# Three instructions of ScalarE's attention stage put in another place of its queue

## The chip, the cores and the metric

One core of a Trainium2 chip runs the whole program. The metric is device time in microseconds (us), median of the runs. Five engines work beside each other, each through its own list of instructions in order: PE (matmuls and transposes, with PEld for its weight loads), DVE, ACT (ScalarE), POOL and SP. They wait for one another by counting semaphores.

## The reference

The input is x, 2048 tokens of 128 features. Two layers are computed, and the change is in the second:

```
xn = layernorm(x)
x  = x + attention(xn) + ffn(xn)                    # layer 1
  attention: q, k with a rotary half; s = q k^T, causal mask; p = softmax(s); o = p v; o wo
  ffn: h = silu(xn w1^T s1) * (xn w2^T s2)          # the gate, 512 wide
       h = gelu(h h1^T sh1); h = gelu(h h2^T sh2); h w3^T s3
```

Layer 0 (a recurrent memory, and one expert) comes first and is not touched.

## The kernel before

The second layer has two stages. The attention stage runs from about 93 to 193 us of the trace, the two 512 x 512 layers and the last one after it. The attention stage is one loop over t = 0 to 16 on every engine (NT = 16). Row t is a block of 128 queries. Its scores go in groups of four key blocks (up to 512 columns, `groups_of`), so rows 8 to 11 have three groups and rows 12 to 15 four; the last one can be shorter (row 8: 512, 512, 128; row 9: 512, 512, 256). In step t the engines do this, in this order:

- PE: the scores of row t (L906), then for row t - 1 the transposes of its first two groups ("turn round", L919), then the matmuls of this step's early gates (L879, L880), then for each group of row t - 1 the product with the values ("weighted", L929), with the turn round of the third group after the first weighted group and of the fourth after the second, then a late gate's matmuls.
- DVE: the maxima of row t's groups (L2022), the negative maximum as bias (L2029), the early gates (L2007, L2008, and from the ninth step on a cast L2014 of its own), then row t - 1: sum, reciprocal, and x += o (L2051), then a late gate, then a check of weights (L2060).
- ACT: the copies of row t - 1's turned groups out of PSUM ("turned copy", L1369), the tanh of the early gates (L1342), the exponentials of row t (L1385, each with a read of its accumulator), casts of early gates (L1397, only for steps before 8), the tanh of a late gate, and pieces of weight conversion (L1357, L1362, L1363).
- POOL: the low half of each gate (L1497, L1498), and weights.

A gate u is one of 32 pieces of 128 x 256. Steps 2 to 11 have two early gates each, steps 6 to 9 one late gate each. So gates 0 and 1 are step 2, gates 17, 18 and late 19 are step 9, gates 22 and 23 are step 11. Gates before 24 take turns in PSUM banks 3 and 6, and PE waits before a gate for the last gate in its bank (`hA_ready`, which L2008 counts up): gate 19 waits for gate 17. From row 12 (`FULL`) on bank 3 belongs to the scores, and PE's scores of row 12 wait for all 24 gates:

```
if t == FULL:

    pe.wait_ge(hA_ready, GATES_AT[FULL])
```

An exponential waits for its bias, and overwrites nothing that PE still needs; scores wait for the exponential that last read their bank. A weighted group waits for its turned copy. DVE's gate waits for its tanh. POOL's part of a gate waits for its cast.

Of the kernel before, what the change touches and what calls it, by code (L numbers as in the profile page):

```python
# [7 lines left out]
ACT = mybir.ActivationFunctionType  # L8
# [25 lines left out]
HT4 = HID // P  # L34
ROT = 64
ZC = 256
# [52 lines left out]
def program(nc, a, out):  # L89
    with ExitStack() as ctx:  # L90
# [3 lines left out]
        def sem(name):  # L94
            return ctx.enter_context(nc.semaphore(name))
# [126 lines left out]
        def second(n):  # L222
            b_at[0] += n
            return arena[:, b_at[0] - n:b_at[0]]
# [12 lines left out]
        hAH, hAL, hBH, hBL = (h[:, i * HT4 * T // 2:(i + 1) * HT4 * T // 2].bitcast(F16).rearrange("p (m t) -> p m t", m=HT4)  # L237
                              for h in (hAf, hBf) for i in range(2))
# [10 lines left out]
        TH, ZA, ZG, zd = gate_[0:3], gate_[3:6] + [second(ZC) for _ in range(3)], gate_[6], gate_[7]  # L249
        NZ = len(ZA)  # L250
# [10 lines left out]
        def weights_with(t):  # L261

            return [i for i in range(NWT) if WT_TILE[i] == t]
# [54 lines left out]
        z_done, tanh_ready, hA_ready = sem("z_done"), sem("tanh_ready"), sem("hA_ready")  # L318
# [3 lines left out]
        w16_ready, xh_act, xl_ready, gate_high, gate_low, wsq_act, wc_ready, tern_ready, rest_ready, low_ready = (  # L322
            sem(n) for n in ("w16_ready", "xh_act", "xl_ready", "gate_high", "gate_low", "wsq_act", "wc_ready", "tern_ready", "rest_ready", "low_ready"))
# [10 lines left out]
        def groups_of(t):  # L334
            before = sum((u + 4) // 4 for u in range(t))
            return [(before + k, c, min(4, t + 1 - c)) for k, c in enumerate(range(0, t + 1, 4))]


        FULL = 3 * NT // 4
        SCORE_BANK = [gi % (3 if t < FULL else 4) for t in range(NT) for gi, _, _ in groups_of(t)]  # L340
        SCORE_AFTER = [max([w for w in range(gi) if SCORE_BANK[w] == SCORE_BANK[gi]], default=None) for gi in range(len(SCORE_BANK))]

# [4 lines left out]
        GATE_EARLY = [range(u, u + n) for u, n in zip(GATES_AT, EARLY_GATES)]  # L347
# [3 lines left out]
        HIGH_BY_ACT = {u for t in range(HIGH_TILES) for u in GATE_EARLY[t]}  # L351
# [77 lines left out]
        def _(sp):  # L429
# [30 lines left out]
            for k, (_, n0, cnt) in enumerate(RESULTS):  # L460
                if k == BY_ACT:
                    continue
                sp.wait_ge(out_ready, k + 1)
                sp.dma_start(out_dram[:, n0:n0 + cnt, :], fin[:, n0:n0 + cnt, :]).then_inc(out_sem, 16)
# [575 lines left out]
        def _(act):  # L1040
            f = nc.scalar.activation
# [255 lines left out]
            def high(c):  # L1297

                f(xH[:, c * BANK:(c + 1) * BANK], xT[:, c * BANK:(c + 1) * BANK], ACT.Copy).then_inc(xh_act, 1)
# [35 lines left out]
            def tanh(u):  # L1335

                act.wait_ge(z_done, u + 1)
                if u == 0:
                    act.wait_ge(scales_ready, 2)
                if u >= 3:  # L1340
                    act.wait_ge(hA_ready, u - 2)
                f(TH[u % 3], PS[:, GATE_BANK[u], 0:ZC], ACT.Tanh, scale=s1h[:, u % HT4:u % HT4 + 1]).then_inc(tanh_ready, 1)  # L1342

            def weights(i):

                if i in (3, 7):
                    act.wait_ge(h_in[(i - 3) // 4], 16)
                if i == 0:

                    act.wait_ge(turned_dve, 4)  # L1350
                    act.wait_ge(turned_pool, 4)
                    act.wait_ge(xl_ready, 4)
                if i >= NWC:

                    act.wait_ge(tern_ready, i - NWC + 1)
                w = weights_of(i)
                f(WC[i % NWC], w, ACT.Square).then_inc(wsq_act, 1)  # L1357
                if i >= 2:
                    k = (i - 3) % 4
                    wH, wL = (q.rearrange("p m e -> p (m e)") for q in (w3H, w3L)) if i == 2 else (  # L1360
                        q[:, k, :] for q in ((h1H, h1L), (h2H, h2L))[(i - 3) // 4])
                    f(wH, w, ACT.Copy).then_inc(w16_ready, 1)  # L1362
                    f(wL, w, ACT.Copy, scale=1.0 / LOW).then_inc(w16_ready, 1)  # L1363

            def turned_back(t):

                for gi, c, cnt in groups_of(t):
                    act.wait_ge(pt_done, gi + 1)
                    f(PT[t % 2][:, c * P:(c + cnt) * P], PS[:, 4 + gi % 2, 0:cnt * P], ACT.Copy).then_inc(pt_act, 1)  # L1369
                    yield  # L1370

            for t in range(NT + 1):
                copies = turned_back(t - 1) if t else iter(())
                next(copies, None)
                next(copies, None)
                for u in GATE_EARLY[t]:
                    tanh(u)
                if t < NT:
                    if t >= 2:
                        act.wait_ge(pv_done, t - 1)  # L1380
                    act.wait_ge(bias_ready, t + 1)
                    for k, (gi, c, cnt) in enumerate(groups_of(t)):
                        if k >= 1:
                            next(copies, None)
                        f(Pr[t % 2][:, c * P:(c + cnt) * P], PS[:, SCORE_BANK[gi], 0:cnt * P], ACT.Exp,  # L1385
                          scale=1.0 / D, bias=nbs[:, t:t + 1], accum_out=rsums[:, gi:gi + 1]).then_inc(p_ready, 1)
                for _ in copies:
                    pass
                if t < 2:
                    high(t + 2)  # L1390
                for u in GATE_EARLY[t]:
                    if u in HIGH_BY_ACT:

                        act.wait_ge(hA_ready, u + 1)
                        if u:
                            act.wait_ge(gate_high, u)
                        f(hAH[:, u % HT4, u // HT4 * ZC:(u // HT4 + 1) * ZC], ZA[u % NZ], ACT.Copy).then_inc(gate_high, 1)  # L1397
                for u in GATE_LATE[t]:
                    tanh(u)
                for i in weights_with(t):  # L1400
                    weights(i)
# [749 lines left out]
```

## Time and profile before

| | |
|---|---|
| median of 3 runs | 256.38 us (256.31 to 256.75) |
| profiled execution, and its span | 256.91 us, 255.1 us |
| PE busy | 245.0 us (96%), 1669 instructions |
| DVE busy | 204.5 us (80%) |
| ACT busy | 185.8 us (73%), 460 instructions |
| POOL busy | 115.0 us (45%) |
| chain that ended last | PE 63%, DVE 20%, POOL 6%, ACT 3%, issue 3%, DMA 2% |
| granted TensorE clock | 1.0 over the span |

The span is the time from the first to the last instruction of one profiled execution; 1.8 us of its own time lie around it. The chain is followed back from the last instruction through whatever released each step.

### The profile page before, as it was taken

The page shows a single profiled execution, that of the slowest core. Times are in us where ns is not written, and L with a number is a line of the kernel's source. Part 1 is how long each engine was busy: PE and PEld are TensorE (multiplying, and loading weights), DVE is VectorE, ACT ScalarE, POOL GpSimd, SP SyncE. Part 2 cuts the span into 40 slices and gives each one's busy share as a digit, 9 for nine tenths or more (in the row PEclk, how much of TensorE's full clock was granted, in tenths as well). Part 3 has the DMA queues.
Part 4 walks back from the last instruction along what each step waited for, and adds up shares of the span by engine and source line. Part 5 has one row for each costly group of instructions (what it writes and reads, how often), then busy time and mean ns, then how long its engine had stood idle before and what let it go on. Part 6 is the DMA issues. An engine that isn't in the chain of part 4 may idle for free.

```text
span 255.1 us, 5149 instructions
## 1 busy us (share of the span) xinstructions
PE 245.0 (96%) x1669; PEld 160.1 (63%) x1673; DVE 204.5 (80%) x681; ACT 185.8 (73%) x460; POOL 115.0 (45%) x150
## 2 busy tenths in 40 slices
PE   7899998999998999999999999999999999999993
PEld 2359554776764477786778767886875444444492
DVE  7888899999958998998899887787613996666674
ACT  2697789976637887887667899989814997777730
POOL 9789700000004589887755994997790000000000
PEclk9999999999999999999999999999999999999999
DMA  6620000000008403000000000000000000000004
GB/s 189 187 81 3 1 0 3 1 0 3 3 3 321 177 15 149 3 1 0 4 0 3 0 0 3 1 1 0 4 3 0 0 0 3 0 1 0 1 29 141
DMA packets 8479, 8.50 MB, mean 33 GB/s; under 512 B 1793, under 2 KB 7554, under 8 KB 7938
## 3 DMA queue, kind: packets, MB, share of 16 engines
q1 hardware_dynamic: 7074, 7.52, 8.8%
q10 hardware_dynamic: 1376, 0.62, 0.9%
q8 instruction: 15, 0.25, 0.4%
q14 instruction: 14, 0.11, 0.1%
HBM read 7.09 MB, written 1.05 MB: 32 GB/s over the span
## 4 chain that ended last, share of the span: by engine, by line
PE 63%; DVE 20%; POOL 6%; ACT 3%; issue 3%; DMA 2%; DVEq 0%; SPq 0%; POOLq 0%; ACTq 0%
PE PS L957 11%; PE PS L956 11%; PE PS L929 8%; PE PS L906 7%; PE PS L919 4%; POOL arena L1497 3%; POOL arena L1498 3%; PE PS L718 3%; DMA x<-L_attn_x 2%; PE PS L672 2%; PE PS L726 2%; DVE mxb L2022 2%; DVE arena L2008 2%; PE PS L575 2%; PE PS L570 2%
## 5 line engine op out<-in xcount | busy, mean ns | idle before, releaser
L956 PE MATMUL PS<-arena 128*128 128x512 f16 x128 | 48.5, 379 | 0.0
L957 PE MATMUL PS<-arena 128*128 128x512 f16 x128 | 48.5, 379 | 0.0
L2080 DVE TENSOR_TENSOR arena<-arena 128x512 f32<-128x512 f32 x32 | 22.2, 693 | 13.0 <-ACT arena L1416 13.0
L906 PE MATMUL PS<-arena 128*128 128x512 f32 (+3 forms) x80 | 31.9, 530 | 0.3 <-ACT arena L1385 0.3
L1415 ACT ACTIVATE arena<-PS,arena 128x512 f32<-128x512 f32 x32 | 22.9, 715 | 9.1 <-PE PS L957 9.1
L1497 POOL TENSOR_TENSOR arena<-arena 128x256 f32<-128x256 f32 x32 | 21.5, 672 | 15.7 <-DVE arena L2014 13.1
L1385 ACT ACTIVATE arena<-PS,lnt 128x512 f32<-128x512 f32 (+3 forms) x40 | 24.8, 628 | 3.2 <-DVE lnt L2029 3.2
L1498 POOL TENSOR_TENSOR arena<-arena,small 128x256 f16<-128x256 f32 (+1 forms) x36 | 23.8, 660 | 2.8
L1505 POOL CAST arena<-arena 128x512 f16<-128x512 f32 x2 | 1.3, 637 | 49.1 <-ACT x L1278 49.1
L1416 ACT ACTIVATE arena<-PS,arena 128x512 f16<-128x512 f32 x32 | 22.8, 712 | 0.0
L2022 DVE TENSOR_REDUCE mxb<-PS 128x1 f32<-128x512 f32 (+3 forms) x40 | 22.1, 601 | 0.0
L957 PEld LDWEIGHTS PS<-arena 128*128 128x128 f16 x128 | 12.5, 98 | 14.7
L956 PEld LDWEIGHTS PS<-arena 128*128 128x128 f16 x128 | 12.5, 98 | 14.6
L906 PEld LDWEIGHTS PS<-arena 128*128 128x128 f32 x80 | 14.0, 191 | 12.0 <-issue 9.8
L919 PE MATMUL PS<-con,arena 128*128 128x128 f32 x136 | 19.5, 273 | 0.0
L929 PE MATMUL PS<-arena,xn 128*128 128x128 f32 x144 | 19.3, 278 | 0.0
L929 PEld LDWEIGHTS PS<-arena,xn 128*128 128x128 f32 x144 | 17.7, 191 | 1.1 <-ACT xn L1369 0.4
L929 PE MATMUL PS<-arena 128*128 128x128 f32 x128 | 17.4, 279 | 0.6 <-ACT arena L1369 0.6
L2051 DVE SCALAR_TENSOR_TENSOR x<-PS,lnt,x 128x128 f32<-128x128 f32 x16 | 5.6, 351 | 14.1 <-PE PS L929 13.7
L919 PEld LDWEIGHTS PS<-con,arena 128*128 128x128 f32 x136 | 15.1, 141 | 2.7 <-issue 1.9
L929 PEld LDWEIGHTS PS<-arena 128*128 128x128 f32 x128 | 15.6, 191 | 1.4 <-ACT arena L1369 1.0
L2008 DVE SCALAR_TENSOR_TENSOR arena<-PS,arena 128x256 f32<-128x256 f32 x32 | 15.5, 484 | 1.1
(292 smaller groups left out, 614.5 us busy)
## 6 DMA issues: line engine op xcount, KB each, us to landing
arena<-h_T SPq DMA_DIRECT2D x2, 1024.0 KB, 5.9
arena<-cos SPq DMA_DIRECT2D x1, 1024.0 KB, 4.8
arena<-sin SPq DMA_DIRECT2D x1, 1024.0 KB, 6.8
arena<-w_T SPq DMA_DIRECT2D x3, 256.0 KB, 3.1
x<-L_attn_x SPq DMA_DIRECT2D x2, 256.0 KB, 5.5
out<-arena SPq DMA_DIRECT2D x2, 256.0 KB, 2.2
x<-L_attn_x SPq DMA_DIRECT2D x2, 128.0 KB, 2.6
x<-L_attn_x ACTq DMA_DIRECT2D x2, 128.0 KB, 3.2
```

What stands on the lines that cost most here:

```text
L906: i = mm(PS[:, k, 0:cnt * P], qT1[:, t * P:(t + 1) * P], kT1[:, c * P:(c + cnt) * P], start=True, stop=not last)
L919: i = tr(PS[:, 4 + gi % 2, (b - c) * P:(b - c + 1) * P], Pr[t % 2][:, b * P:(b + 1) * P], ident)
L929: i = mm(PS[:, 7, (t % 4) * D:(t % 4 + 1) * D], PT[t % 2][:, b * P:(b + 1) * P], V1[:, b, :], start=(b == 0), stop=(b == t))
L956: mm(bank(b), wH[:, k, m * P:(m + 1) * P], sH[:, k, cols], start=(k == 0), stop=False)
L957: i = mm(bank(b), wL[:, k, m * P:(m + 1) * P], sL[:, k, cols], start=False, stop=(k == HT4 - 1))
L1385: f(Pr[t % 2][:, c * P:(c + cnt) * P], PS[:, SCORE_BANK[gi], 0:cnt * P], ACT.Exp, scale=1.0 / D, bias=nbs[:, t:t + 1], accum_out=rsums[:, ...
L1415: f(FP[u % 4], bank(u % 8), ACT.Gelu, scale=s_[:, u % HT4:u % HT4 + 1])
L1416: f(high, bank(u % 8), ACT.Gelu, scale=s_[:, u % HT4:u % HT4 + 1]).then_inc(read, 1)
L1497: o.need(o.did(tt(rest, value, high, ALU.subtract)))
L1498: return tt(low, rest, low_scale.broadcast_to([P, cols]), ALU.mult)
L2022: i = did(v.tensor_reduce(mxb[:, gi:gi + 1], PS[:, SCORE_BANK[gi], 0:cnt * P], AX.X, ALU.max))
L2080: v.tensor_tensor(RP[m], FP[m], high, ALU.subtract).then_inc(rest_ready, 1)
```

## The change

All three edits are on ACT, and nothing is added or removed: the same 460 instructions run in another order.

1. The cast of gate 1 (`HIGH_LATER = 2`, the second early gate of step 2) stood at the end of step 2. It now stands in step 3, behind the turned copy of row 2.
2. In step 9 (`COPY_FIRST`) the third turned copy of row 8 (128 columns) stood behind the first exponential of row 9. It now stands behind the first two copies, ahead of the tanhs of gates 17 and 18 and of all three exponentials.
3. In step 11 (`TANH_LATER`) the tanh of gate 23 stood behind that of gate 22 and ahead of the exponentials. It now stands behind the third exponential of row 11.

```
+            def high_of_gate(u):
+
+                if u in HIGH_BY_ACT:
+                    act.wait_ge(hA_ready, u + 1)
+                    if u:
+                        act.wait_ge(gate_high, u)
+                    f(hAH[:, u % HT4, u // HT4 * ZC:(u // HT4 + 1) * ZC], ZA[u % NZ], ACT.Copy).then_inc(gate_high, 1)
+
+            HIGH_LATER, COPY_FIRST, TANH_LATER = 2, 9, 11
+
             for t in range(NT + 1):
                 copies = turned_back(t - 1) if t else iter(())
                 next(copies, None)
                 next(copies, None)
-                for u in GATE_EARLY[t]:
+                if t == COPY_FIRST:
+                    next(copies, None)
+                if t == HIGH_LATER + 1:
+                    high_of_gate(GATE_EARLY[HIGH_LATER][-1])
+                behind = 1 if t == TANH_LATER else len(GATE_EARLY[t])
+                for u in GATE_EARLY[t][:behind]:
                     tanh(u)
                 if t < NT:
...
                 for _ in copies:
                     pass
+                for u in GATE_EARLY[t][behind:]:
+                    tanh(u)
                 if t < 2:
                     high(t + 2)
                 for u in GATE_EARLY[t]:
-                    if u in HIGH_BY_ACT:
...
+                    if t != HIGH_LATER or u != GATE_EARLY[t][-1]:
+                        high_of_gate(u)
```

## Rows read from the trace of the kernel before

**Rows 1.** Windows: busy us of each engine in a stretch, then granted clock.
```profile
93.00:132.00 39.00, 38.67 (x276) 30.66 (x277) 35.22 (x100) 28.88 (x80) 31.66 (x43) 1.00 0.08 28
132.00:148.00 16.00, 15.33 (x104) 11.90 (x103) 13.96 (x38) 13.32 (x36) 11.49 (x15) 1.00 0.00 1
148.00:190.00 42.00, 42.00 (x281) 32.51 (x281) 29.39 (x75) 35.02 (x83) 33.91 (x38) 1.00 0.01 1
190.00:249.00 59.00, 59.00 (x356) 30.61 (x355) 41.26 (x79) 40.54 (x65) 1.24 (x1) 1.00 0.02 5
```
**Rows 2.** Chain that ended last, in order: start, us, what.
```profile
132.71 0.49 PE PS L929 x2
...
146.48 1.35 ACT arena L1385 x4
...
147.83 3.04 PE PS L906 x8
```
**Rows 3.** Timeline, step 3: start, us, engine, line, what, count, [idle before <-releaser].
```profile
100.65 0.42 ACT L1397 ACTIVATE arena<-arena 128x256 f16<-128x256 f32 x1 [0.63 <-DVE arena L2008]
100.97 0.47 ACT L1369 ACTIVATE arena<-PS 128x384 f32<-128x384 f32 x1
101.49 0.74 PEld L929 LDWEIGHTS PS<-arena 128*128 128x128 f32 x6 [0.49 <-ACT arena L1369]
101.70 0.15 DVE L2029 TENSOR_SCALAR lnt<-mxb 128x1 f32<-128x1 f32 x1
101.84 0.42 DVE L2007 SCALAR_TENSOR_TENSOR arena<-arena,PS 128x256 f32<-128x256 f32 x1
```
**Rows 4.** Timeline of ACT, step 9.
```profile
130.16 0.84 ACT L1342 ACTIVATE arena<-PS,arena 128x256 f32<-128x256 f32 x2
131.71 0.69 ACT L1385 ACTIVATE arena<-PS,lnt 128x512 f32<-128x512 f32 x1 [0.71 <-DVE lnt L2029]
...
132.39 0.27 ACT L1369 ACTIVATE arena<-PS 128x128 f32<-128x128 f32 x1
132.55 0.69 ACT L1385 ACTIVATE arena<-PS,lnt 128x512 f32<-128x512 f32 x1
```
**Rows 5.** Groups by line and form, 90 to 190 us: busy us, mean ns.
```profile
L1342 ACT ACTIVATE arena<-PS,arena 128x256 f32<-128x256 f32 x32 | 14.2, 480 | 0.1
```
**Rows 6.** Timeline of PE and its weight loads, step 9.
```profile
131.19 0.27 PE L919 MATMUL PS<-con,arena 128*128 128x128 f32 x1
...
132.71 0.30 PEld L929 LDWEIGHTS PS<-arena 128*128 128x128 f32 x2 [0.54 <-ACT arena L1369]
...
133.04 0.27 PE L879 MATMUL PS<-arena 128*128 128x256 f16 x1
```
**Rows 7.** Timeline of DVE, steps 9 and 10.
```profile
131.46 0.15 DVE L2029 TENSOR_SCALAR lnt<-lnt 128x1 f32<-128x1 f32 x1
131.58 0.42 DVE L2007 SCALAR_TENSOR_TENSOR arena<-arena,PS 128x256 f32<-128x256 f32 x1
132.04 0.48 DVE L2008 SCALAR_TENSOR_TENSOR arena<-PS,arena 128x256 f32<-128x256 f32 x1
```
**Rows 8.** Timeline of ACT and the weight loads, step 10.
```profile
138.53 0.69 ACT L1385 ACTIVATE arena<-PS,lnt 128x512 f32<-128x512 f32 x1 [0.18 <-DVE lnt L2029]
...
139.21 0.37 ACT L1369 ACTIVATE xn<-PS 128x256 f32<-128x256 f32 x1
...
138.65 1.50 PEld L929 LDWEIGHTS PS<-arena,xn 128*128 128x128 f32 x12
```
**Rows 9.** Timeline of ACT, step 11.
```profile
144.43 0.84 ACT L1342 ACTIVATE arena<-PS,arena 128x256 f32<-128x256 f32 x2
145.14 0.71 ACT L1385 ACTIVATE arena<-PS,lnt 128x512 f32<-128x512 f32 x1
...
147.70 0.64 ACT L1357 ACTIVATE arena<-arena 128x512 f32<-128x512 f32 x1
```
**Rows 10.** Timeline of DVE and the weight loads, steps 11 and 12.
```profile
144.94 0.42 DVE L2007 SCALAR_TENSOR_TENSOR arena<-arena,PS 128x256 f32<-128x256 f32 x1 [0.80 <-ACT arena L1342]
...
147.09 0.48 DVE L2008 SCALAR_TENSOR_TENSOR arena<-PS,arena 128x256 f32<-128x256 f32 x1
...
147.80 0.30 PEld L906 LDWEIGHTS PS<-arena 128*128 128x128 f32 x2 [0.48 <-issue]
```

More of the change, by code:

```diff
@@ L1391, in _ @@
                 for u in GATE_EARLY[t]:
-                    if u in HIGH_BY_ACT:
[L1394 to L1397, printed above, removed]
+                    if t != HIGH_LATER or u != GATE_EARLY[t][-1]:
+                        high_of_gate(u)
                 for u in GATE_LATE[t]:
```

## The prediction

> **What bounds the kernel now.** I read the stretches first: they say which engine has no room where the three edits stand. From 93 to 132 us DVE is busy 35.22 of 39 us and PE's rows overlap, so its 38.67 says little; from 148 us to the end of the second 512-wide layer PE is busy 42.00 of 42.00 and 59.00 of 59.00 us, without a gap [rows 1]. So whatever delays or advances PE at about 148 us moves the end by the same amount, and an edit before 132 us counts only if DVE or the hand-over to PE moves. Then I read the chain of waits in order of time. It changes from DVE to PE at 132.71 us, at the third weighted group of row 8, and at 147.83 us it enters the scores of row 12, after which it stays on PE [rows 2]. Last I read the timelines around the three places; the working below is a re-timing from them.
>
> **Edit 1, gate 1's cast behind row 2's copy: 0 to -0.1 us, I take -0.03.** Before, the cast waited 0.63 us for DVE and the copy stood behind it at 100.97 us [rows 3]. The copy's input is there at about 100.3 us, so it starts some 0.65 us earlier, the cast follows at about 100.7, where it was anyway, and the tanhs and PE's weighted group move up by some 0.4 us. PE had idled 0.49 us there [rows 3]. What takes over is DVE: gate 2 starts 0.14 us after its bias instruction at 101.70 [rows 3], and every later pair of these is 0.11 to 0.15 apart as well (0.12 in step 9 [rows 7]), so at most 0.03 us was a wait for the tanh. DVE has no other gap to give until step 6. PE is early, then waits for nothing it could not have had. The cast is no later, so nothing queued behind it (two tanhs and an exponential) is either.
>
> The chain names POOL between 97 and 114 us, which I don't follow: a gate waits for POOL's part of the gate six before it, and that was done 3 to 5 us earlier each time.
>
> **Edit 2, row 8's short copy ahead of the tanhs: +0.58 us.** What it removes: the copy at 132.39 us stood behind an exponential that waited for its bias, and PE idled 0.54 us for it, until 132.71 [rows 4, 6]. What it adds: the copy can't start before its transpose, a matmul at 131.19 of 0.27 us [rows 6], so 131.50 with the 0.04 us that such a hand-over takes. In front of that point ACT used to run both tanhs, from 130.16 on [rows 4]; they now stand in the queue behind the waiting copy, and behind them all of row 9's exponentials.
> - Copy 131.50; it holds the queue 0.16 us, as from 132.39 to 132.55 [rows 4]. The tanh of gate 17 is at 131.66 and takes 0.48 us [rows 5], to 132.13.
> - DVE's gate 17 was at 131.58, straight behind the bias [rows 7]. It now waits until 132.16: +0.58 us. It is ready 0.94 us on (0.46 to the second instruction, which takes 0.48 [rows 7]), at 133.10.
> - The second tanh is 0.36 us behind the first (0.84 less 0.48 [rows 4, 5]), and the first exponential 0.36 behind that: 132.38 in place of 131.71 [rows 4], +0.67.
> - PE gets the copy at 131.8, runs the third weighted group without its stall at 132.2, and then stands before gate 19, which waits for gate 17: 133.16 in place of 133.04 [rows 6]. The 0.54 us are gone and PE is 0.12 us later than before.
> - DVE runs the rest of step 9 and the maxima of row 10 without a gap, so the +0.58 stays: row 10's bias, and with it the exponential that waits for it at 138.53, moves to 139.11, and row 9's third copy, behind that, from 139.21 to 139.79 [rows 8].
> - PE needs that copy for the last four of twelve weight loads. They take 1.50 us where eight take 0.97 and four more 0.44: it already waited some 0.09 us for it [rows 8]. So here PE falls back the full 0.58 us.
> Bounds: +0.12 if DVE makes its delay good within row 10 (its cast of gate 18 ran 0.63 us in place of 0.29 beside POOL, which is such a place), +0.67 if the exponential's shift counts. I take 0.58, the first one that has no slack behind it.
>
> The Trainium skill, "ScalarE: Activation LUTs", Rules for kernel authors, has a budget of about 0.3 us for every ACTIVATE and 0.83 ns for an element. By it the copy would hold the queue 0.41 and the tanh 0.51 us, gate 17 would start at 132.45, and the edit would cost 0.87 us and the whole change 2.4. The trace overlaps neighbours (0.16 and 0.36 from start to start), and I stay with it.
>
> **Edit 3, gate 23's tanh behind row 11's exponentials: +1.57 us.** Before, the two tanhs ran from 144.43 and the first exponential from 145.14 [rows 9]. Without the second tanh that exponential starts 0.36 us earlier, which buys nothing: the copy behind it waits for its transpose until 145.95, so the second and third exponentials stay. The tanh goes to where the third exponential lets go of the queue, the 147.70 of the next instruction [rows 9], and ends at 148.17. DVE had gate 22 at 144.94, 0.03 us behind its tanh [rows 10]; gate 23 so starts at 148.20 and is ready at 149.14, where it was ready at 147.09 + 0.48 = 147.57 [rows 10]. The scores of row 12 wait by the code for 24 gates, this one the last; they came at 147.80, 0.23 us behind it [rows 10]. They now come at 149.37: +1.57. PE's whole queue is behind them (rows 12 to 15, then both layers), as are DVE's row 10 output and weight checks behind the gate; the weight conversions on ACT move 0.36 us and had idled 0.5 us in front of the next copy. PE is the bound from there on [rows 1], with nothing that gives time back. Bounds: the same 1.57 less the 0.23 if that was not hand-over, so +1.34, and +1.8 if the cast that follows, and runs beside POOL, holds DVE longer.
>
> **Sum.** Edit 3's path starts from PE's transposes of row 10, so edit 2's delay adds to it: -0.03 + 0.58 + 1.57 = +2.12 us. From the profiled execution's 256.91 us (span 255.1) that gives 259.0 (span 257.2). The median shown is 0.53 us below the profiled one, so I forecast 256.38 + 2.12 = 258.5 us. Its own range is 258.1 to 258.9.
>
> **The rivals.**
> - *Only edit 3 costs (18%).* DVE makes up for step 9 in steps 10 and 11 (it idles 0.80 us in step 11 [rows 10]), and PE keeps up to all of the 0.54 us it wins [rows 6], or loses 0.12. For it: the idle time is there. Against it: the hand-over in step 10 comes before that idle time. Time: 256.38 + 1.57 - 0.54 = 257.4 up to 256.38 + 1.57 + 0.12 = 258.1.
> - *Not slower: row 12's scores don't hang on gate 23 (6%).* The chain puts the start at 147.83 down to the exponentials of row 11, 1.35 us of them up to that moment [rows 2]. If the exponentials decide, then the one at 145.14 coming 0.36 us earlier and the stall of 0.54 us taken away are both wins: 256.38 - 0.36 - 0.54 = 255.5, at best; with edit 2's loss, 256.6. The point from which it decides is whether the tanh is done before the exponentials are. Against it: the code waits for the count of 24, and the banks of row 12's first scores were read by an exponential two us earlier.
> - *The clock falls (3%).* PE now stands idle from about 148.1 to 149.95 us, longer than any gap in the stretches shown, in all of which the granted clock was 1.00 [rows 1]. If it came back from there at 1.2 GHz, row 12's step (147.83 to 155.7) would take up to 7.9 us more, 266 at worst. The Trainium skill, "TensorE: Matmul & The Clock Gate", section "HAM oscillation", says that gaps of idle time send the array back to the lower clock; no gap in this trace shows it, so it has this small chance.
> - *Something larger in edit 2 (the rest of the slower side).* As by the exponential's 0.67 or more, to 259.2.
> That the change doesn't do what it says has no case of its own, but edit 2 is such in part: the copy is put ahead of the tanhs too, and they are what is costly.
>
> **How the numbers follow.** The forecast's mechanism 67%, only edit 3 18%, larger 6%, clock 3%, not slower 6%. A difference of 0.2% is 0.5 us, about what can be told from none. Slower by more than that: 94%. The case that isn't slower splits into 3% within 0.2% and 3% faster. The range takes the forecast's own, most of the rival without edit 2's cost, and the larger case: 257.5 to 259.1.
>
> **What would show it.** Step 3: the weight load of row 2's weighted group starts near 101.1 and gate 2 at 101.8. Step 9: the short copy at 131.5 with idle time for PE's transpose in front of it, tanhs behind it, DVE's gate 17 at 132.16 with a wait for ACT, PE's third weighted group without a stall and then a new one of 0.7 us before gate 19. Step 10: PE waits some 0.5 us in row 9's last weighted group. Step 11: DVE idle for some 2 us before gate 23, PE idle for as long before row 12's scores, which start near 149.95. Behind it the same durations, all 2.1 us later. I am wrong if row 12's scores start at 148.5 or earlier, if PE between 148 and the end has idle time that takes some of it back, or if DVE's gate 17 is not late.

## The result, and the profile after

The changed kernel takes 259.31 us (median of 4 executions, 259.14 to 260.84) where the kernel before took 256.55 beside it: ratio 1.0114, interval 1.0076 to 1.0153. Measured again on another occasion it is 258.59 us (6 executions, 258.50 to 260.19) over 256.67, ratio 1.0088 (1.0063 to 1.0112). It is slower, as forecast. The forecast was 258.5 with a range up to 259.1, so the first median lies 0.2 us above the range, and the second within it. The profiled execution took 259.17 us, span 257.4, where the prediction's working had 259.0 and 257.2.

Windows first, of the changed kernel, cut so that they match [rows 1]: start:end, length, then busy us of PE, weight loads, DVE, ACT and POOL, and the granted clock. The stretch from step 9 to row 12's scores is 18.15 us where it was 16.00, with PE's busy time unchanged (15.35 against 15.33); behind it PE is full as before.

```profile
132.00:150.15 18.15, 15.35 (x104) 11.75 (x103) 14.48 (x38) 15.04 (x39) 12.69 (x16) 1.00 0.00 1
150.15:192.30 42.15, 42.15 (x282) 32.64 (x283) 29.31 (x74) 33.85 (x81) 32.77 (x36) 1.00 0.00 1
192.30:251.30 59.00, 59.00 (x356) 30.63 (x356) 41.29 (x79) 40.62 (x65) 1.19 (x1) 1.00 0.02 6
```

Step 3 of the changed kernel, to hold against [rows 3]: the copy has moved from 100.97 to 100.24, PE's weighted group from 101.49 to 101.13 without a stall, and DVE's gate 2 only from 101.84 to 101.78.

```profile
100.24 0.49 ACT L1369 ACTIVATE arena<-PS 128x384 f32<-128x384 f32 x1 [0.23 <-PE PS L919]
100.64 0.42 ACT L1378 ACTIVATE arena<-arena 128x256 f16<-128x256 f32 x1
...
101.13 0.74 PEld L929 LDWEIGHTS PS<-arena 128*128 128x128 f32 x6
...
101.78 0.42 DVE L2020 SCALAR_TENSOR_TENSOR arena<-arena,PS 128x256 f32<-128x256 f32 x1
```

Step 9 and 10 of the changed kernel on ACT (lines 1 to 5), DVE (6) and the weight loads (7 to 10), to hold against [rows 4, 6 to 8]. The short copy now waits 1.23 us for PE with the tanhs behind it. DVE's gate 17 waits for its tanh. PE's last weighted group of row 8 runs straight on (ten loads in a row), and then the weight loads stand 0.78 us before gate 19 (the matmuls themselves 0.59). In step 10 the loads stand 0.46 us for row 9's third copy (the matmuls 0.27).

```profile
131.49 0.28 ACT L1369 ACTIVATE arena<-PS 128x128 f32<-128x128 f32 x1 [1.23 <-PE PS L919]
131.66 0.83 ACT L1342 ACTIVATE arena<-PS,arena 128x256 f32<-128x256 f32 x2
132.38 0.70 ACT L1400 ACTIVATE arena<-PS,lnt 128x512 f32<-128x512 f32 x1
...
139.12 0.69 ACT L1400 ACTIVATE arena<-PS,lnt 128x512 f32<-128x512 f32 x1 [0.63 <-DVE lnt L2042]
...
139.80 0.37 ACT L1369 ACTIVATE xn<-PS 128x256 f32<-128x256 f32 x1
...
132.16 0.42 DVE L2020 SCALAR_TENSOR_TENSOR arena<-arena,PS 128x256 f32<-128x256 f32 x1 [0.55 <-ACT arena L1342]
...
131.18 1.20 PEld L929 LDWEIGHTS PS<-arena 128*128 128x128 f32 x10
133.16 0.10 PEld L879 LDWEIGHTS PS<-arena 128*128 128x128 f16 x1 [0.78 <-DVE arena L2021]
...
138.79 0.97 PEld L929 LDWEIGHTS PS<-arena,xn 128*128 128x128 f32 x8
140.22 0.52 PEld L929 LDWEIGHTS PS<-arena,xn 128*128 128x128 f32 x4 [0.46 <-ACT xn L1369]
```

Step 11 of the changed kernel on ACT, DVE and the weight loads, to hold against [rows 9, 10]. The tanh of gate 23 is at 148.29, DVE idles 1.47 us before the gate, and row 12's scores start at 150.01 behind 2.10 us without a weight load.

```profile
145.02 0.48 ACT L1342 ACTIVATE arena<-PS,arena 128x256 f32<-128x256 f32 x1
...
148.29 0.48 ACT L1342 ACTIVATE arena<-PS,arena 128x256 f32<-128x256 f32 x1
...
146.57 0.76 DVE L2027 CAST arena<-arena 128x256 f16<-128x256 f32 x1
148.80 0.42 DVE L2020 SCALAR_TENSOR_TENSOR arena<-arena,PS 128x256 f32<-128x256 f32 x1 [1.47 <-ACT arena L1342]
149.26 0.48 DVE L2021 SCALAR_TENSOR_TENSOR arena<-PS,arena 128x256 f32<-128x256 f32 x1
...
150.01 0.30 PEld L906 LDWEIGHTS PS<-arena 128*128 128x128 f32 x2 [2.10 <-issue]
```

### The profile page after: what moved, and what is told of

Same layout as the page of the kernel before. It is cut to its first block, busy times and chain, and to the rows that moved or that the text cites. A ratio compares the mean times of both kernels' runs of the same rounds, so it can differ in the third digit from the quotient of the medians.

```text
span 257.4 us, 5153 instructions
## 1 busy us (share of the span) xinstructions
PE 244.9 (95%) x1673; PEld 159.9 (62%) x1673; DVE 204.7 (80%) x681; ACT 186.1 (72%) x460; POOL 115.2 (45%) x150
## 4 chain that ended last, share of the span: by engine, by line
PE 64%; DVE 19%; POOL 6%; ACT 3%; issue 2%; DMA 2%; DVEq 0%; SPq 0%; POOLq 0%; ACTq 0%
PE PS L956 11%; PE PS L957 11%; PE PS L929 8%; PE PS L906 8%; PE PS L919 4%; POOL arena L1510 3%; POOL arena L1511 3%; PE PS L718 3%; PE PS L672 2%; DMA x<-L_attn_x 2%; PE PS L726 2%; PE PS L575 1%; PE PS L570 1%; PE PS L879 1%; PE PS L710 1%
## 5 line engine op out<-in xcount | busy, mean ns | idle before, releaser
L906 PEld LDWEIGHTS PS<-arena 128*128 128x128 f32 x80 | 14.0, 191 | 13.6 <-issue 11.4
L2020 DVE SCALAR_TENSOR_TENSOR arena<-arena,PS 128x256 f32<-128x256 f32 x32 | 13.4, 420 | 5.2 <-ACT arena L1342 4.4
L1369 ACT ACTIVATE xn<-PS 128x512 f32<-128x512 f32 (+1 forms) x20 | 10.4, 552 | 9.0 <-PE PS L919 9.0
```

The costliest lines, as they stand in the source:

```text
L906: i = mm(PS[:, k, 0:cnt * P], qT1[:, t * P:(t + 1) * P], kT1[:, c * P:(c + cnt) * P], start=True, stop=not last)
```

## The experiments

The profiled executions differ by up to 1 us in when they begin the attention stage, though no edit stands ahead of it (0.5 us between the two profiles of the changed kernel). To take that out, each profile is read from one instruction, the accumulator read behind row 0's exponential (at 93.92 us before, at 93.91 in the changed kernel, 93.11 to 94.14 over all profiles); times counted from it are called times by the common clock. "To row 12" is the time from there to the first weight load of row 12's scores, "rest" from that load to the start of the last addition on DVE, which ends the chain's work there.

| kernel | median, us | median before beside it | ratio (interval) | to row 12 | rest |
|---|---|---|---|---|---|
| before | | | | 53.88 | 103.66 |
| changed | 259.31 | 256.55 | 1.0114 (1.0076 to 1.0153) | 56.10 | 103.69 |
| changed, again | 258.59 | 256.67 | 1.0088 (1.0063 to 1.0112) | 56.03 | 103.66 |
| edit 1 alone | 256.81 | 256.67 | 1.0003 (0.9990 to 1.0015) | 53.89 | 103.69 |
| edit 2 alone | 257.27 | 256.67 | 1.0019 (1.0009 to 1.0029) | 54.51 | 103.67 |
| edit 3 alone | 259.83 | 256.67 | 1.0121 (1.0101 to 1.0140) | 55.49 | 105.36 |
| edit 3, gap filled | 258.38 | 256.90 | 1.0062 (1.0049 to 1.0076) | 55.32 | 103.68 |
| changed, gap filled | 258.99 | 256.90 | 1.0086 (1.0072 to 1.0100) | 55.85 | 103.67 |
| tanh behind second exponential | 257.80 | 256.90 | 1.0039 (1.0026 to 1.0053) | 54.81 | 103.67 |
| tanh behind first exponential | 256.74 | 256.77 | 0.9999 (0.9988 to 1.0011) | 53.90 | 103.66 |
| copies behind tanhs | 256.98 | 256.90 | 1.0002 (0.9993 to 1.0011) | 53.90 | 103.68 |
| casts later | 256.62 | 256.77 | 0.9997 (0.9987 to 1.0007) | 53.35 | 103.93 |
| copies and casts | 256.25 | 256.77 | 0.9973 (0.9960 to 0.9987) | 52.87 | 104.04 |

**The three edits one by one.** Each sets the constants of the other two out of reach:

```
-            HIGH_LATER, COPY_FIRST, TANH_LATER = 2, 9, 11
+            HIGH_LATER, COPY_FIRST, TANH_LATER = 2, 99, 99      # likewise 99, 9, 99 and 99, 99, 11
```

> Only edit 1 on the kernel before: gate 1's cast behind row 2's copy. Theory (ScalarE's order is free there, DVE is the bound): gate 2 on DVE 0 to 0.06 us earlier, time within 0.1 us of before. Rival (PE's removed stall of 0.49 us in step 3 counts): 0.3 to 0.4 us faster.

> Only edit 2 on the kernel before: row 8's third copy ahead of the tanhs and exponentials of step 9. Theory: DVE's gate 17 at 132.16 in place of 131.58, PE's last weighted group of row 9 0.58 us late, row 12's scores and the end +0.6 us. Rival (DVE makes it good in steps 10 and 11): row 12's scores -0.4 to +0.12 us.

> Only edit 3 on the kernel before: gate 23's tanh behind row 11's exponentials. Theory (row 12's scores hang on gate 23): they start 1.6 us late and so does the end. Rival (they hang on the exponentials): no later than before, 0 to -0.4 us.

> The changed kernel once more, on one chip with its three parts. If the parts add: the sum of the three differences, +2.2 us by the two profiles. The medians so far differ by 2.76 us, of which the profiled executions show 2.26. If the rest is real work it shows in every round and in the spans; if it is scatter of single executions, the median difference here is 2.2 to 2.4 us. A lower granted clock in some executions would show in their clock figure.

Edit 1 is worth nothing: 0.01 us in the profile, no difference in the ratio that can be told from none, and the rival's 0.3 us faster lies outside its interval. Edit 2 costs 0.63 us up to row 12 and 0.49 us by the ratio; the rival by which DVE makes it good is out. Edit 3 delays row 12 by 1.61 us, and the rival by which the exponentials decide is out. The three add to 2.25 in the profiles, and the changed kernel has 2.22 and 2.15. But edit 3 alone costs 3.1 us by its ratio: its "rest" is 1.70 us longer, which no theory on the order of the queue has. Here is where it lies, in windows of PE alone for edit 3 alone (length, busy us, granted clock), and the matmuls of row 12's scores behind a gap of 1.90 us, which took 4.73 us where the changed kernel's profiled execution has 3.03:

```profile
149.00:149.50 0.50, 0.16 (x1) 1.00 0.00 0
149.50:150.00 0.50, 0.50 (x1) 0.65 0.00 0
150.00:150.50 0.50, 0.50 (x2) 0.50 0.00 0
...
152.50:153.00 0.50, 0.50 (x2) 0.50 0.00 0
153.00:153.50 0.50, 0.50 (x2) 0.94 0.00 0
153.50:154.00 0.50, 0.50 (x5) 1.00 0.00 0
```

```profile
149.34 4.73 PE L906 MATMUL PS<-arena 128*128 128x512 f32 x8 [1.90 <-DVE arena L2021]
```

```profile
150.04 3.03 PE L906 MATMUL PS<-arena 128*128 128x512 f32 x8 [1.94 <-DVE arena L2021]
```

The granted clock fell to its lower level, 1.2 GHz, some 0.3 us after PE came back, and returned 3.4 us later. All five executions of edit 3 alone show a mean clock of 0.989 to 0.993 and times from 259.53 us on. (The mean also counts the end of the span, when PE has finished and the level is lower again, so the profiled executions without a fall in the middle have 0.996 to 1.000.) Of the changed kernel's ten executions two do: 260.84 and 260.19 us, both at 0.993, where the other eight lie between 258.50 and 259.45.

**The gap filled.** Does the idle time cost the clock?

```
                 if t == FULL:
+                    keep_warm(8, 4)          # 8 matmuls of 512 columns on constants, result not used
                     pe.wait_ge(hA_ready, GATES_AT[FULL])
```

> Edit 3 alone, with eight matmuls of 512 columns on constants (some 0.22 us each, 1.7 us) put into PE's gap ahead of its wait for gate 23; their result is not used. Theory (the idle gap lets the clock fall): row 12's scores start at the same place, 1.6 us late, granted clock 1.00 throughout, time 1.6 us over before, that is 1.6 us less than edit 3 alone. Rival (the lower clock has another cause, or the 3.2 us are no matter of clock): as edit 3 alone, 3.2 us over before.

> The changed kernel with the same eight matmuls in the gap. Theory: 2.1 to 2.3 us over before in every execution, none 1.6 us higher. Rival: one execution in four to six stays 1.6 us higher, as now.

With the gap filled, edit 3 alone costs 1.6 us by its ratio, 1.5 less than without, and the clock is 0.999 to 1.000 in all five executions. So in edit 3 alone the idle time is the cause of the fall. The changed kernel's five filled executions lie between 258.94 and 259.18; with two high ones in ten before, that alone would prove little. There was a small thing besides, in the weight loads of edit 3 with the gap filled: the scores follow gate 23 by 0.17 us less than behind an idle gap (55.32 against 55.49 by the common clock, with the gate ready at the same 55.26). The changed kernel shows the same (0.05 us behind the gate with the gap filled, 0.23 and 0.27 without). So part of the 0.23 us in [rows 10] is what PE takes to set off again after standing idle.

```profile
147.14 1.50 PEld L513 LDWEIGHTS PS<-warm 128*128 128x128 bf16 x8
149.11 0.30 PEld L906 LDWEIGHTS PS<-arena 128*128 128x128 f32 x2 [0.46 <-DVE arena L2021]
```

**The tanh one and two exponentials earlier.** In the loop over the exponentials instead of behind it:

```
                           scale=1.0 / D, bias=nbs[:, t:t + 1], accum_out=rsums[:, gi:gi + 1]).then_inc(p_ready, 1)
+                        if t == TANH_LATER and k == 1:       # k == 0 in the other
+                            tanh(GATE_EARLY[t][-1])
```

> Edit 3 alone, but gate 23's tanh behind the second of row 11's three exponentials. Theory: tanh at 147.04, gate 23 ready at 148.5, row 12's scores 0.9 us late, time +0.9 us if the clock holds over a gap of 1.3 us, up to +2.6 if it falls in all executions. Rival (the scores hang on the last exponential, which is 0.36 us later): +0.4 us.

> Edit 3 alone, but gate 23's tanh behind the first of row 11's exponentials, in ScalarE's idle time ahead of the third copy. Theory (gate 23 is free until DVE is through with gate 22's cast, which ends with POOL's weight operation near 146.7): no change, within 0.1 us, where the same tanh behind the second exponential cost 0.9 us. Rival (any tanh taken from its place costs): +0.3 to +0.6 us.

Behind the first, second and third exponential the same tanh costs 0.02, 0.93 and 1.61 us up to row 12. The first is free: ACT had 0.41 us of idle time there (edit 3 leaves it open in front of the third copy), and DVE, which had gate 22's cast to finish, came to gate 23 only 0.7 us after the tanh was done. Behind the second PE stands idle for 1.2 us, and the clock of row 12 stayed at 1.00. The profile's 0.93 and the ratio's 1.0 us agree.

**The copy behind the tanhs.** Is it the copy or the tanhs behind it that cost edit 2 its time?

```
                 for u in GATE_EARLY[t]:
                     tanh(u)
+                if t in (9, 10):
+                    next(copies, None)
```

> The kernel before with the third turned copy of steps 9 and 10 behind the tanhs and ahead of the first exponential. Theory (edit 2 lost by the tanhs, not by the copy): gate 17 stays where it was, PE's stall of 0.54 us ahead of the last weighted group shrinks by 0.35 us, the hand-over in step 10 goes the same way, row 12's scores and the end 0.35 us earlier. Rival (the exponential behind the copy of step 10, 0.33 us late, delays row 11's scores): 0 to +0.3 us.

Edit 2's loss is gone, but the expected 0.35 us didn't come: 0.02 us to row 12, ratio 1.0002. (Step 10's copy was moved as well, so this run doesn't price step 9's alone.) PE is indeed ahead, by 0.45 us at the end of row 10's last weighted group: the rows below are of this kernel, and row 12's scores now come behind 0.95 us without a load, where it was 0.48 [rows 10]. What holds them is a cast on DVE (first line), 1.21 us long where it was 0.75, which ends 0.15 us behind a POOL operation (second line, 144.77 + 1.27 = 146.04) that started before it. Gate 23 stands behind that cast, ready at 53.67 us by the common clock, where it was 53.65.

```profile
144.98 1.21 DVE L2016 CAST arena<-arena 128x256 f16<-128x256 f32 x1
...
144.77 1.27 POOL L1534 TENSOR_TENSOR arena<-arena 128x512 f32<-128x512 f32 x1
...
147.26 0.30 PEld L906 LDWEIGHTS PS<-arena 128*128 128x128 f32 x2 [0.95 <-issue]
```

**The casts later, alone and with the copies.** If the cast is what holds row 12, both gates should go first:

```
                 for u in GATE_EARLY[t]:
                     gate(u)                  # without its cast in step 11
+                for u in GATE_EARLY[t]:
+                    if u in CAST_LATER:      # gates 22 and 23
+                        cast(u)
```

> The kernel before with DVE's casts of gates 22 and 23 behind both gates of step 11. Theory (row 12's scores hang on gate 23, and gate 23 on gate 22's cast, which lasts until POOL's operation ends): gate 23 ready at 146.9 in place of 147.57, row 12's scores as soon as PE is free, 0.45 us earlier, and the end with them. Rival (the scores hang on the exponentials of row 11): 0.

> The kernel before with the third copies of steps 9 and 10 behind the tanhs and ahead of the first exponential, and with DVE's casts of step 11 behind both gates. Theory: in the kernel with the copies alone PE was 0.45 us early ahead of row 12's scores and lost it in a gap of 0.95 us before gate 23. With the casts out of the way both count, 0.9 us faster. Rival (another wait takes their place, such as the bank of row 12's third group, last read by the last exponential of row 11): 0.45 us faster, as with the casts alone.

With the casts later row 12 comes 0.53 us earlier, straight behind PE's work (no gap at its first load); but 0.27 us are given back, and the expected 0.45 us at the end didn't come: by the ratio nothing is left that can be told. In its timeline ACT waits for row 12's bias from DVE, where before it did not, and in step 13 PE waits for a turned copy (0.26 and then 0.15 us). Part of the cause is the edit itself: run one behind the other (last row below), DVE's two casts end later than the two had before, so the sum behind them starts at 54.44 us by the common clock where it was 54.08, and row 12's bias is ready at 58.73 where it was 58.36. The exponential then starts at 58.82, where it was 58.81, though PE is 0.5 us ahead.

```profile
146.95 0.30 PEld L906 LDWEIGHTS PS<-arena 128*128 128x128 f32 x2
...
159.39 0.97 PEld L929 LDWEIGHTS PS<-arena 128*128 128x128 f32 x8 [0.26 <-ACT arena L1369]
```

```profile
152.42 0.69 ACT L1385 ACTIVATE arena<-PS,lnt 128x512 f32<-128x512 f32 x1 [0.41 <-DVE lnt L2033]
...
146.55 1.58 DVE L2003 CAST arena<-arena 128x256 f16<-128x256 f32 x2
```

With both, row 12 is 1.01 us earlier, 0.38 are given back, and the kernel is a little faster than the one before: 256.25 against 256.77 us, ratio 0.9973 (0.9960 to 0.9987), some 0.7 us where 0.9 was expected. The rival by which the last exponential's bank takes over is out, since row 12 would then have come only some 0.5 us earlier.

## Why the prediction was right or wrong

- *What bounds the kernel*: right. From row 12's scores to the end all kernels need 103.66 to 103.69 us, unless the clock falls or PE comes early enough for DVE to be late.
- *Edit 1, 0 to -0.1*: right. The 0.4 us at PE's stall came (101.49 to 101.13) and were of no use; DVE's gate moved 0.06, where the working had allowed 0.03.
- *Edit 2, +0.58*: right in every place (gate 17 at 132.16, gate 19 at 133.16, the third copy 0.59 us later), 0.63 measured up to row 12. The reading that the tanhs cost it and not the copy is shown by the kernel with the copy behind them. The trace also decides against the 0.87 us that was worked out from the budget in the Trainium skill, "ScalarE: Activation LUTs", Rules for kernel authors: from the copy's start to the first tanh's it is 0.17 us and not 0.41.
- *Edit 3, +1.57*: right on what row 12 hangs on, 1.61 measured up to row 12, and the steps of 0.02, 0.93 and 1.61 follow the tanh. Incomplete on what the gap does besides. One of its signs was misread: DVE was to be idle for some 2 us before gate 23, and is for 1.47, since gate 22's cast runs 0.76 us into that time (0.75 before).
- *Sum for the profiled execution, 259.0*: 259.17.
- *From there to the median*: this step failed. "The median shown is 0.53 us below the profiled one" was carried over to the changed kernel as if a profiled execution always lay that much above its median. It does not: here the profiled 259.17 us lie 0.14 below the median. The miss of 0.81 us (259.31 against 258.5) is these 0.53 + 0.14, and another 0.14 by which the profiled execution exceeds the working's 259.03. What the 0.53 was is scatter, for the greater part of the start. In the changed kernel's two profiled executions (259.17 and 258.56 us) the chain's first load of x takes 5.36 us in one and 4.86 in the other, and everything after it shifts alike (common instruction at 93.91 and 93.39):

```profile
1.72 5.36 DMA x<-L_attn_x
```

```profile
1.72 4.86 DMA x<-L_attn_x
```

  The kernel before has executions from 256.10 to 257.50 us (and one more, at 257.99), with medians of 256.55, 256.67, 256.90 and 256.77 where the forecast stood on 256.38. The range of the forecast's own, 0.8 us wide, is narrower than this scatter. So it is luck too that the second median, 258.59, is within 0.1 us of the forecast. The execution of 260.84 us with the lower clock isn't what decided: without it the first median is 259.17, still above 259.1.
- *The clock falls, 3%*: this rival was judged too small. It was ruled nearly out because no gap in the trace before had cost the clock, but none there had been as long as 1.9 us. It happened in all five executions of edit 3 alone and, by their times and clock, in two of the changed kernel's ten, one of them among the first four. Its price, 1.7 us, is far under the 7.9 us taken as worst. With what the Trainium skill says in "TensorE: Matmul & The Clock Gate", section "HAM oscillation", that gaps of idle time send the array back to the lower clock, the trace of edit 3 alone agrees (the lower level behind a gap of 1.90 us); the two profiled executions of the changed kernel, with gaps of 1.94 and 1.90 us and the clock at 1.00 behind them, do not.
- *Only edit 3 costs*, *not slower*: both out, by edits 2 and 3 alone.

Open: why the same gap of 1.9 us costs the clock in all five executions of edit 3 alone, and in the changed kernel in two of ten at most. By the common clock the two differ by 0.6 us in when it comes; but counted from the start of the trace it comes at 147.44 us in edit 3 alone and at 147.55 in the changed kernel's second profile, where the clock held, so that is no explanation yet. The two high executions of the changed kernel were not profiled; that it is the same fall there is inferred from their clock of 0.993 and the 1.6 us. The kernel before, without such a gap, has one execution like them among 67, of 257.99 us at 0.993 (the others have 0.995 to 1.000), not profiled either. So it is not shown that the gap is what makes the changed kernel's rare ones.

## What to carry to other kernels

An instruction moved ahead in an in-order queue is judged by what stands behind it while it waits: the short copy removed a stall of 0.54 us and put two tanhs and three exponentials behind a wait of 1.23. Before an instruction is moved back, look in the code for whoever needs its result last, and don't go by the name in the chain of waits, which put row 12's start down to the exponentials [rows 2]: the same tanh was free behind the first exponential and cost 0.9 and 1.6 us behind the second and third. And a new idle gap on TensorE can have a second price beside its length, which a run that fills the gap will show.

## What was not expected of the hardware

- A gap of 1.9 us on TensorE was followed by some 3.4 us at the lower of the two clock levels, worth 1.7 us, in all five executions of edit 3 alone, and in the changed kernel in neither of two profiled ones and perhaps in two of ten; a gap of 1.2 us was not, in five executions.
- A cast of f32 to f16 on DVE (0.29 us alone) that started while POOL was in a 512-wide tensor operation ended 0.15 us after that operation, in 0.40, 0.75 or 1.21 us. DVE's gate operations, which have two tensor operands of which one lies in PSUM, kept their 0.42 and 0.48 us beside the same POOL operations.
- TensorE's first weight load of row 12 came 0.05 us after gate 23 was ready when TensorE had been kept busy until then (two profiles), and 0.23 us after it when it had stood idle (eight of nine profiles, 0.27 in the other).
